# The norm factor of the gated outputs moves from ScalarE ahead of the output projection to VectorE behind it

## The reference, cut to what matters

```python
og = o * _silu(z)
og = og * jax.lax.rsqrt(jnp.mean(og * og, axis=-1, keepdims=True) + EPS) * norm_weight
return og.reshape(Bv, Tv, VDIM) @ W_out
```

## Time and profile before

| | us |
|---|---|
| Runs of the kernel before, median of 3 | 1365.02 (1362.15 to 1374.51) |
| The profiled execution, its own time | 1363.42 |
| Its span from the first to the last instruction | 1361.7 |
| PE busy | 1206.6 |
| DVE busy | 941.5 |
| ACT busy | 825.3 |
| POOL busy | 724.5 |
| Mean granted clock of PE | 0.95 of full |

### The profile page before, as it was taken

One profiled execution on the slowest core, in us unless ns is written; L12 is line 12 of the kernel. 1 busy time (PEld: TensorE's weight loads), 2 busy tenths in 40 slices (PEclk: granted clock), 3 DMA queues, 4 the chain that ended last, 5 costly groups with the idle time before them and its releaser, 6 DMA issues. The chain is left out here.

```text
span 1361.7 us, 30307 instructions
## 1 busy us (share of the span) xinstructions
PE 1206.6 (89%) x10704; PEld 1010.3 (74%) x10704; DVE 941.5 (69%) x2293; ACT 825.3 (61%) x2269; POOL 724.5 (53%) x1171
## 2 busy tenths in 40 slices
PE   7788999999999999999999999999987889978774
PEld 6677788887888788777878788878877777745453
DVE  6786878787878878787878787888753223224776
ACT  6235676666767666767666676766664643126871
POOL 3285766767575858576676757585856010020001
PEclk8687999999999999999999999999998988988997
DMA  4214041312122230404131212222050200000003
GB/s 166 77 33 105 8 103 23 86 33 76 35 75 44 67 84 26 105 6 105 22 88 32 78 36 73 43 68 60 11 136 17 53 1 0 0 1 1 1 2 96
DMA packets 138630, 70.71 MB, mean 52 GB/s; under 512 B 112456, under 2 KB 128336, under 8 KB 136560
## 3 DMA queue, kind: packets, MB, share of 16 engines
q1 hardware_dynamic: 138480, 68.78, 19.8%
HBM read 54.97 MB, written 13.76 MB: 50 GB/s over the span
## 5 line engine op out<-in xcount | busy, mean ns | idle before, releaser
L1041 POOL TENSOR_TENSOR tmp<-Dm,Tn 64x31 f32<-64x31 f32 (+15 forms) x496 | 260.4, 525 | 87.9 <-DMA Dm<-blk_in_scratch 52.6
L1044 POOL TENSOR_TENSOR Tn<-Tn,tmp 64x31 f32<-64x31 f32 (+15 forms) x496 | 286.2, 577 | 38.9
L853 DVE SCALAR_TENSOR_TENSOR cv<-bank,cw,cv 128x255 f32<-128x255 f32 (+2 forms) x384 | 155.0, 472 | 77.4 <-ACT cv L649 77.4
L1017 POOL TENSOR_TENSOR ro<-ss,mhalf 128x4 f32<-128x4 f32 x64 | 65.1, 1018 | 244.3 <-ACT junk L711 207.0
L853 DVE SCALAR_TENSOR_TENSOR cqk<-bank,cw,cqk 128x255 f32<-128x255 f32 (+2 forms) x384 | 154.8, 471 | 10.0 <-ACT cqk L649 10.0
L461 PE MATMUL bank<-wo,OTs 128*128 128x256 f32 x512 | 136.5, 400 | 11.6 <-ACT OTs L742 11.6
L913 DVE SCALAR_TENSOR_TENSOR BP<-bank,cj,E 128x512 f32<-128x512 f32 (+1 forms) x256 | 142.8, 611 | 2.5 <-DVE cj L898 0.3
L711 ACT ACTIVATE junk<-og 128x129 f32<-128x129 f32 x256 | 79.9, 312 | 97.9 <-issue 81.2
L917 DVE TENSOR_TENSOR R<-Vs,bank 128x256 f32<-128x256 f32 x64 | 26.9, 421 | 134.2 <-PE bank L427 134.2
L461 PEld LDWEIGHTS bank<-wo,OTs 128*128 128x128 f32 x512 | 91.9, 194 | 26.1 <-ACT OTs L742 15.0
L719 ACT ACTIVATE ogn<-og,ro 128x128 f32<-128x128 f32 x256 | 81.9, 398 | 28.7 <-POOL ro L1017 28.6
(11 more groups left out here) (213 smaller groups left out, 3473.3 us busy)
## 6 DMA issues: line engine op xcount, KB each, us to landing
rvz<-in_L_attn_W_qkvz SPq DMA_DIRECT2D x16, 512.0 KB, 5.0
x<-alpha_scratch SPq DMA_DIRECT2D x8, 1024.0 KB, 6.3
alb<-alpha_scratch SPq DMA_DIRECT2D x7, 1024.0 KB, 6.4
rqk<-in_L_attn_W_qkvz SPq DMA_DIRECT2D x16, 256.0 KB, 2.6
wo<-in_L_attn_W_out SPq DMA_DIRECT2D x16, 256.0 KB, 5.3
blk_in_scratch<-BP SPq DMA_DIRECT2D x256, 16.0 KB, 1.5
tinv_scratch<-Tn SPq DMA_DIRECT2D x32, 128.0 KB, 2.2
tinv_t_scratch<-Tt SPq DMA_DIRECT2D x32, 128.0 KB, 2.2
```

The costliest lines, as they stand in the source:

```text
L853: nc.vector.scalar_tensor_tensor(d, bk[:, t * T:(t + 1) * T - s], cw[p][:, first + t, TAPS - 1 - s:TAPS - s], d, ALU.mult, ALU.add).then_i ...
L1041: pool_step_done(nc.gpsimd.tensor_tensor(t, Dm[:, j, j + 1:BLK].unsqueeze(2).broadcast_to([SLOTS, r, c]), Tn[:, j, 0:c].unsqueeze(1).broad ...
L1044: pool_step_done(nc.gpsimd.tensor_tensor(Tn[:, j + 1:BLK, 0:c], Tn[:, j + 1:BLK, 0:c], t, ALU.subtract), kh * NTS + 2 * j + 4)
```

## The change

PE turns og itself. ogn and `act_ogn` are gone. `pe_f` no longer accumulates the two heads: for one chunk it puts head 0's product in columns 0 to 255 of bF and head 1's in 256 to 511, so that a chunk fills the bank, and f of chunk 1 has to wait until DVE has taken chunk 0. `dve_acc` is called once for each chunk and adds each head's 256 columns, multiplied by ro, to acc in an instruction of its own; the second of them waits for the first. f of chunk 1 moves: in merge steps from between merge 2 and merge 3 to behind solve 1, in the others from ahead of z to behind it, which makes it the step's last work on PE. On DVE, acc 1 stands behind r2 and ahead of the weight split and scans in merge steps, and at the very end of the step in the others.

```diff
             def pe_ot(kh, p, b, scaled):
-                wait(nc.tensor, "ogn", at(kh, b, 4, 4))
+                wait(nc.tensor, "og", at(kh, b, 2, 2))
...
-                        last = nc.tensor.transpose(bOT[:, n * P:(n + 1) * P], ogn[:, c, h, :], ident)
+                        last = nc.tensor.transpose(bOT[:, n * P:(n + 1) * P], og[b % 2][:, c, h, 0:DK], ident)
...
             def pe_f(kh, p, b, c):
+
                 if c == 0:
                     wait(nc.tensor, "ots", at(kh, b, 1, 1))
-                    wait(nc.tensor, "acc", at(kh, b, 1))
                     if b == 0:
                         wait(nc.tensor, "wo_in", (kh + 1) * 16)
+                wait(nc.tensor, "acc", at(kh, b, 4, 2 * c))
                 for h in range(R):
-                    last = nc.tensor.matmul(bF[:, c * D:(c + 1) * D], OTs[:, h, c, :], wo[p][:, h, :],
-                                            start=(h == 0), stop=(h == R - 1))
-                if c == 1:
-                    last.then_inc(sem("f"), 1)
+                    last = nc.tensor.matmul(bF[:, h * D:(h + 1) * D], OTs[:, h, c, :], wo[p][:, h, :], start=True, stop=True)
+                last.then_inc(sem("f"), 1)
...
                     pe_merge(kh, p, b, 2)
-                    if last:
-                        pe_f(*last, 1)
                     pe_merge(kh, p, b, 3)
...
                     pe_solve(kh, p, b, 1)
+                    if last:
+                        pe_f(*last, 1)
                     if vt:
                         pe_vt(*vt, now)
...
                     pe_f(*last, 0)
-                    pe_f(*last, 1)
                     if vz:
                         pe_z(*vz, 0)
                         pe_z(*vz, 1)
+                    pe_f(*last, 1)
...
-            def act_ogn(kh, p, b):
-                wait(nc.scalar, "ro", at(kh, b, 1, 1))
-                wait(nc.scalar, "ot", at(kh, b, 1))
-                for c in range(NC):
-                    for h in range(R):
-                        n = c * R + h
-                        nc.scalar.activation(ogn[:, c, h, :], og[b % 2][:, c, h, 0:DK], ACT.Copy, scale=ro[b % 2][:, n:n + 1]).then_inc(sem("ogn"), 1)
-
...
-            def dve_acc(kh, p, b):
-                wait(nc.vector, "f", at(kh, b, 1, 1))
-                a = acc[:, NC * b:NC * (b + 1), :].rearrange("p c d -> p (c d)")
-                wait(nc.vector, "acc", at(kh, b, 1, 1 - B))
-                nc.vector.tensor_tensor(a, a, bF[:], ALU.add).then_inc(sem("acc"), 1)
+            def dve_acc(kh, p, b, c):
+                wait(nc.vector, "f", at(kh, b, 2, c + 1))
+                wait(nc.vector, "ro", at(kh, b, 1, 1))
+                a = acc[:, NC * b + c, :]
+                for h in range(R):
+                    wait(nc.vector, "acc", at(kh, b, 4, c * R + h))
+                    nc.vector.scalar_tensor_tensor(a, bF[:, h * D:(h + 1) * D], ro[b % 2][:, c * R + h:c * R + h + 1], a,
+                                                   ALU.mult, ALU.add).then_inc(sem("acc"), 1)
...
-                if last:
-                    dve_acc(*last)
                 if merges(b):
+                    if last:
+                        dve_acc(*last, 0)
                     dve_r2(kh, p, b)
+                    if last:
+                        dve_acc(*last, 1)
+                    splits(kh, p, b, dve_split_qk, dve_split_vz)
                 else:
                     dve_og(kh, p, b)
-                splits(kh, p, b, dve_split_qk, dve_split_vz)
+                    dve_acc(*last, 0)
+                    splits(kh, p, b, dve_split_qk, dve_split_vz)
+                    dve_acc(*last, 1)
...
                 pe_ot(NKH - 1, 1, B - 1, 2 * NG)
-                pe_gate_up(0, 2)
-                for c in range(NC):
-                    pe_f(NKH - 1, 1, B - 1, c)
-                for m in range(3, HT):
+                for m in range(2, HT):
                     pe_gate_up(0, m)
+                    if m < 4:
+                        pe_f(NKH - 1, 1, B - 1, m - 2)
...
-                dve_acc(NKH - 1, 1, B - 1)
+                dve_acc(NKH - 1, 1, B - 1, 0)
                 ln_norm(dve, 1, 2)
+                dve_acc(NKH - 1, 1, B - 1, 1)
```

More of the change, by code:

```diff
@@ L255, in build @@
             og = [sb(f"og{i}", [P, NC, R, DK + 1], ctx=s1) for i in range(2)]
-            ogn = sb("ogn", [P, NC, R, DK], ctx=s1)
             junk = sb("junk", [P, DK + 1], ctx=s1)
@@ L739, in act_ots @@
                 wait(nc.scalar, "ot", at(kh, b, 1, 1))
-                wait(nc.scalar, "f", at(kh, b, 1))
+                wait(nc.scalar, "f", at(kh, b, 2))
                 wait(nc.scalar, "nw_scaled", 1)
@@ L800, in act_step @@
                 if merges(b):
-                    if last:
-                        act_ogn(*last)
                     act_merge(kh, p, b, 0)
@@ L923, in dve_og @@
                     if c == 0:
-                        wait(nc.vector, "ogn", at(kh, b, 4, -4))
+                        wait(nc.vector, "ot", at(kh, b, 1, -1))
+                        wait(nc.vector, "ss", at(kh, b, 4, -4))
                     nc.vector.scalar_tensor_tensor(og[b % 2][:, c, :, 0:DK], bO[:, c * 256:(c + 1) * 256].rearrange("p (h d) -> p h d", h=R),
                                                    vsc[p][:, b, c:c + 1], zs[:, b, c, :].rearrange("p (h d) -> p h d", h=R), ALU.mult, ALU.mult).then_inc(sem("og"), 1)
-            def dve_acc(kh, p, b):
-                wait(nc.vector, "f", at(kh, b, 1, 1))
-                a = acc[:, NC * b:NC * (b + 1), :].rearrange("p c d -> p (c d)")
-                wait(nc.vector, "acc", at(kh, b, 1, 1 - B))
-                nc.vector.tensor_tensor(a, a, bF[:], ALU.add).then_inc(sem("acc"), 1)
+            def dve_acc(kh, p, b, c):
[6 more added lines that the diff above has]
+                                                   ALU.mult, ALU.add).then_inc(sem("acc"), 1)
             def dve_step(kh, p, b):
@@ L1003, in dve_behind @@
                     nc.vector.wait_ge(sem(f"x_in{b - 1}"), 32)
-                    nc.vector.wait_ge(sem("acc"), at(NKH - 1, b, 1))
+                    nc.vector.wait_ge(sem("acc"), at(NKH - 1, b, 4))
                     residual(ch, rt[:], b - 1, acc[:, NC * (b - 1):NC * b, :], 0, 0, "res0a")
@@ L1015, in pool_ro @@
                 wait(nc.gpsimd, "ss", at(kh, b, 4, 4))
-                wait(nc.gpsimd, "ogn", at(kh, b, 4, -4))
+                wait(nc.gpsimd, "acc", at(kh, b, 4, -4))
                 nc.gpsimd.tensor_tensor(ro[b % 2][:], ss[b % 2][:], mhalf[:, 0:4], ALU.pow).then_inc(sem("ro"), 1)
@@ L1082, in sp_load_wo @@
             def sp_load_wo(kh):
-                wait(nc.sync, "f", at(kh - 1, 0, 1))
+                wait(nc.sync, "f", at(kh - 1, 0, 2))
                 nc.sync.dma_start(wo[kh % 2][:], wout_d[kh * R * DK:(kh + 1) * R * DK, :].rearrange("(h p) n -> p h n", p=DK)).then_inc(sem("wo_in"), 16)
@@ L1435, in _ @@
                 place_h(1)
-                act_ogn(NKH - 1, 1, B - 1)
                 act_gate(0, 0)
@@ L1533, in _ @@
                     dve_hact(0, m)
-                dve_acc(NKH - 1, 1, B - 1)
+                dve_acc(NKH - 1, 1, B - 1, 0)
                 ln_norm(dve, 1, 2)
+                dve_acc(NKH - 1, 1, B - 1, 1)
                 dve.wait_ge(sem(f"x_in{B - 1}"), 32)
-                dve.wait_ge(sem("acc"), NG)
+                dve.wait_ge(sem("acc"), 4 * NG)
                 residual(chf, rt[:], B - 1, acc[:, NC * (B - 1):NT, :], 0, 0, "res0a")
```

## The result

| | us |
|---|---|
| Changed kernel, median of 4 runs | 1407.58 (1405.59 to 1413.57) |
| Kernel before, beside it, median of 4 | 1363.59 (1360.55 to 1374.51) |
| Ratio | 1.0315, 95% interval 1.0248 to 1.0382 |
| The profiled execution, its own time and its span | 1413.57, 1411.7 |
| Mean granted clock of PE | 0.932 |

The account below looks back on a forecast made before the run. PE was taken as the bound, DVE nearly as late in b = 3. +2.8 us per head over 14 heads (+39) and -5.2 at the end gave +34 on 1363.4, 1397.4; as a median 1399, range 1362 to 1436.

Parts of the forecast that it names:

- z and f 1 behind the taps of v, and acc 1's place: Steps b = 0 to 3: DVE's later split and f 1 behind z lengthen each head by 2.8 us, +39 over 14.
- X: The start of solve 1 of a step on PE, from which the forecast counts times within the step.
- b = 3: Last step of a head: acc 1 waits for f 1 and delays DVE's queue and z; +0.65 us.
- Merge 3's uncovered wait: Merge steps on PE: with f 1 gone from between merge 2 and merge 3, the 1.06 us there stay, idle.
- The pair of adds: DVE's two dependent adds for a chunk: 0.95 us, bounds 0.78 and 1.2; 1.9 for 0.68 in each step.
- The last two heads and the MLP's start: End of the loop: -9.7 for the saved wait, +1.8 for f 1, +2.7 at the MLP's start; together -5.2 us.
- The clock in the steady part: Rival: PE's clock falls while PE idles ahead of z in two steps a head; +70 us or half; chance 0.09.
- PE stays the bound: Rival: X of b = 2 moves with PE, the whole 43.8 us of waiting are saved, 13.5 paid: 1335 us; chance 0.14.
- Loss and gain nearly cancel: Rival: f 1 costs nothing in merge steps, b = 3 keeps its length; +1.0 us per head, 1374 us; chance 0.15.

Follow-up runs that it names:

- e3: Changed kernel with acc 1 of the merge steps moved from behind r2 to the next step behind og; 1389.60 us, ratio 1.0219.
- e2: Changed kernel's order and waits with the old work (ogn on ACT, heads accumulated, one plain add for each chunk); 1407.60 us, ratio 1.0356.
- e6: As e3, and in steps b = 2 and 3 too acc 1 goes into the next step, behind the first half of bp; 1389.99 us, ratio 1.0208.
- e1: Kernel before with only ogn and its four ACT instructions removed, norm factor ro applied nowhere; 1321.59 us, ratio 0.9726.
- e4: Changed kernel with the four transposes of og repeated uselessly between merge 2 and merge 3 in merge steps; 1391.20 us, ratio 1.0223.
- e5: Changed kernel with half of DVE's adds: head 1's product is projected but not added; 1373.40 us, ratio 1.0086.
- e9: Changed kernel repaired: f 1 again between merges 2 and 3, acc 0 between v's taps, acc 1 later, bp's second half ahead of r2; 1338.44 us, ratio 0.9824.

## Why the prediction was right

By its steps, for the profiled executions, whose spans differ by 50.0 us where I had 34:

- **z and f 1 behind the taps of v, and acc 1's place.** Forecast 2.8 us a head: +0.45, -0.25, +1.93, +0.65. Measured undisturbed: +0.36, -0.34, +1.70, +0.83, together 2.55. z of b = 2 starts at X + 6.69 as foretold, the split starts 2.44 behind solve 1 for my 2.6 and 1.09 before. e3 shows acc 1's place, e2 that the order alone brings 1.9 of the 2.55. This is the mechanism of b = 2, and its size was near: solve 1 comes 0.6 later in its step for my 1.05, and the end 2.66 behind z for my 2.42.
- **b = 3: right in size, wrong in path.** I let acc 1's wait push DVE's whole queue and with it z, to 11.93 behind the step's start for 12.17 in the earlier trace rows. But r2 starts where it did before, DVE idles 0.82 ahead of it, and z comes at 11.79; e6 takes acc 1's wait away and the step keeps its 14.45. The other half of my sum is what costs: z to f 1 1.69 (1.65 foretold), and 0.97 for f 1 (0.77). The two ends lay 0.14 apart, so the figure came out near all the same, which was luck.
- **Merge 3's uncovered wait.** 1.06 foretold between merge 2 and merge 3 without work; 0.83 of it shows as waiting in 32 steps. Right.
- **The pair of adds.** 0.95 foretold, 1.00 measured and 0.92 to the next start; two instructions of og that don't wait for each other take 0.78 to the next start (639.57 to 640.35). So the wait between them costs 0.14. The Trainium skill ("VectorE: DVE Perf Modes", "The DRAIN you can't avoid") has the semaphore cost nothing; in this trace it costs that.
- **The last two heads and the MLP's start: mis-sized.** The term "together -5.2" was -17.8 in the span, from the last Gram matmul on. I had left PE's clock as it was there; it rose from 0.85 to 0.93 of full over that stretch. e1 shows the same, larger.
- **The clock in the steady part: wrong as a rival with 0.09.** I made it a case apart, at +70 or half of that. It came with the forecast's own mechanism: the 55 steps from the second to the last Gram matmul became 64.6 us longer, of which the undisturbed lengths give 35 and the clock the other 29. I also looked for it at z's wait alone; there it does fall in b = 2, but in b = 1 it falls behind two short waits of 0.44 and 0.83 and a row of small matmuls, and e4, which fills that gap, takes most of the falls away in both. This miss of 29 and the one above, 13 the other way, offset each other in part, which is luck and the reason why 1399 stood so near to 1407.58. The rest, 3.3 us, lies ahead of the second step.
- **The rival "PE stays the bound".** e1 reached 1321.59, so its prize exists, but more than half of it lies in the last two heads. Against its 38 us stands e2's order at 48; the two don't add up to the change's 44, since both act on the same steps, and the longer adds (e5) and the clock come in. "Loss and gain nearly cancel" fell with the undisturbed lengths of b = 2 and 3.

## What to carry to other kernels

When work moves to an in-order engine, price its place before its length: list what stands behind the new instruction and its wait, and follow that list to the other engine's next wait. A wait in the profile is worth only what is not late right behind it (e1: 34 us of waiting in the steady part, 17 gained there), and a wait elsewhere in the same step may cover it wholly (e6 against e3: 52 us of DVE's idleness, nothing gained). Once such a change has shown its loss, moving the pieces to where both engines have time can turn it: e9 computes the same as the changed kernel 5% faster, part of which is bp's place.

## What the runs showed of the hardware that was not expected

PE's clock fell to 1.2 GHz for some 3.4 us at a time behind waits no longer than 0.44 and 0.83 us, close together with small matmuls between and after them, while single waits of 1.0 to 1.5 us left it at 2.4 GHz in the kernel before and in e1. Adding 13 us of useless transposes in these gaps made the kernel 13 to 16 us faster (e4). And e5, with the same waits of 0.44, 0.82 and 1.88 us, stayed at full clock from 200 to 900 us in its profiled execution, and its ten executions differ by 18.5 us, the slower ones, on the whole, at lower mean clocks. Which condition makes the clock fall, no run here shows. The Trainium skill ("TensorE: Matmul & The Clock Gate", "A second HAM failure mode: psum-queue depth-cycling") tells of small idle pieces between groups of matmuls that make the clock swing; the changed kernel, e3 and e4 agree with it, the kernel before, with its 3.6 us of waits in each head, and e5, with 6.5, do not.
